# Cross-attention's output projections two tiles ahead of the self-attention turns, and an earlier split of the query weights

## What is computed

```python
x = x + xattn(layernorm(x), ctx)      # 16 heads of 32, q from x, k and v from ctx, softmax, output projection Wo
x = x + attn(layernorm(x))            # qkv projection, rms norm of q and k per head, softmax, projection Wproj
x = x + ffn(layernorm(x))             # token mixing, 9 expert paths, one chosen per token, layernorm
```

## Time and profile before

| | us |
|---|---|
| median of 3 runs | 804.55 (803.83 to 805.03) |
| the profiled execution | 803.47 |
| its span in the trace | 801.9 |
| TensorE matmul busy | 756.4 (94%) |
| VectorE / ScalarE / GpSimd busy | 388.9 / 336.3 / 190.5 |

### The profile page before, as it was taken

One profiled execution on the slowest core, in us unless ns is written; L12 is line 12 of the kernel. 1 busy time (PEld: TensorE's weight loads), 2 busy tenths in 40 slices (PEclk: granted clock), 3 DMA queues, 4 the chain that ended last, 5 costly groups with the idle time before them and its releaser, 6 DMA issues. The chain is left out here.

```text
span 801.9 us, 20594 instructions
## 1 busy us (share of the span) xinstructions
PE 756.4 (94%) x8258; PEld 590.4 (74%) x8258; DVE 388.9 (48%) x941; ACT 336.3 (42%) x690; POOL 190.5 (24%) x246
## 2 busy tenths in 40 slices
PE   5999999999999999999999996699999989999994
PEld 4777778777877887788778774587888766777673
DVE  5644333452444343334433545566667665633446
ACT  4435443544445444435443453334454545521210
POOL 0001010010010010100100202555777760692002
PEclk9999999999999999999999998899999989999998
DMA  8201111011001101110121015120000022100011
GB/s 327 81 36 54 53 54 54 1 52 52 17 36 52 52 0 52 52 52 0 52 52 43 9 52 159 23 73 2 1 0 0 1 68 80 40 0 1 1 54 52
DMA packets 9464, 36.95 MB, mean 46 GB/s; under 512 B 2633, under 2 KB 2889, under 8 KB 6482
## 3 DMA queue, kind: packets, MB, share of 16 engines
q1 hardware_dynamic: 9426, 36.42, 13.4%
HBM read 34.32 MB, written 2.10 MB: 45 GB/s over the span
## 5 line engine op out<-in xcount | busy, mean ns | idle before, releaser
L94 PE MATMUL pj<-W_hi 128*128 128x512 f32 x512 | 209.0, 408 | 9.7 <-DVE W_lo L594 9.7
L96 PE MATMUL pj<-W_lo,W_hi 128*128 128x512 f32 x512 | 200.9, 392 | 0.0
L95 PE MATMUL pj<-W_hi,W_lo 128*128 128x512 f32 x512 | 200.0, 391 | 0.0
L94 PEld LDWEIGHTS pj<-W_hi 128*128 128x128 f32 x512 | 96.6, 189 | 41.0 <-issue 22.6
L96 PEld LDWEIGHTS pj<-W_lo,W_hi 128*128 128x128 f32 x512 | 96.5, 188 | 21.5
L95 PEld LDWEIGHTS pj<-W_hi,W_lo 128*128 128x128 f32 x512 | 96.9, 189 | 17.9
L235 POOL COPY q_b<-Q_T 128x128 f32 (+1 forms) x32 | 9.3, 292 | 415.7 <-PE tp L358 349.0
L492 ACT ACTIVATE K<-pj,bk 128x512 f32<-128x512 f32 x64 | 44.2, 690 | 135.8 <-PE pj L96 135.8
L654 DVE CUSTOM_DVE_ANT_0 m_flat<-sc,mask 128x257 f32<-128x257 f32 x64 | 25.3, 424 | 117.7 <-PE tp L358 94.3
L507 ACT ACTIVATE p_flat<-m_flat,nmax 128x257 f32<-128x257 f32 x128 | 63.8, 501 | 24.6 <-DVE nmax L654 24.5
L499 ACT ACTIVATE V<-pj 128x512 f32<-128x512 f32 x64 | 38.3, 598 | 73.6 <-PE pj L96 71.8
(11 more groups left out here) (271 smaller groups left out, 1337.8 us busy)
## 6 DMA issues: line engine op xcount, KB each, us to landing
raw<-ctx_dram SPq DMA_DIRECT2D x15, 1024.0 KB, 4.8
raw<-w_dram SPq DMA_DIRECT2D x6, 768.0 KB, 4.8
raw<-w_dram SPq DMA_DIRECT2D x4, 1024.0 KB, 4.8
x_nat<-x_dram SPq DMA_DIRECT2D x2, 1024.0 KB, 12.2
out_dram<-raw SPq DMA_DIRECT2D x8, 256.0 KB, 2.1
raw<-wk_dram SPq DMA_DIRECT2D x2, 512.0 KB, 5.7
p_flat<-ctx_dram SPq DMA_DIRECT2D x2, 512.0 KB, 6.9
m_flat<-wv_dram SPq DMA_DIRECT2D x1, 1024.0 KB, 10.3
```

The costliest lines, as they stand in the source:

```text
L94: eng.matmul(out, a_hi, b_hi, start=first, stop=False)
L95: eng.matmul(out, a_lo, b_hi, start=False, stop=False)
L96: return eng.matmul(out, a_hi, b_lo, start=False, stop=last)
```

## The change

- LEAD = 2: `wo_proj` runs for tile it + 2 in turn it. Turn 0 holds `wo_proj` of tiles 0, 1 and 2, turns 1 to 5 that of tiles 3 to 7, turns 6 and 7 none. `o_split` and `o_rest` move with it (tile it + 3 in turn it). Tiles 1 to 3 get halves of their own in `xm_hi`, `xm_lo`, free at that time, and tiles 1, 2 and 3 the banks pw[1], pa[0] and pa[1].
- The low half of tile 1 is made by VectorE (`o1_rest`) instead of GpSimd.
- `x1_stats` is cut in two: `take_x1(t)` (the add into `x_nat`) for tile it + 2, and the statistics for tile it. In turn 0 VectorE's order is: low half of tile 1, take 0, statistics 0, take 1, `weight_split(2)`, take 2.
- In turn 2 the Q projection comes before the q and k transposes on TensorE. In turn 1 VectorE's second `mean_squares` and the V evacuation come before the head norm of q.
- Turns 6 and 7 are written out on TensorE and VectorE; turns 3 to 7 on ScalarE and GpSimd.
- In the last pair of cross-attention, the split of Wq moves ahead: on ScalarE before the first V evacuation, on VectorE between the two `mask_max`.

```diff
@@ cross_attention, scalar, pair
                 k_evac(n, 3)
+                if last:
+                    weight_split(1, 8 * (NPAIR - 1) + 4)
                 v_evac(n, 0)
...
                 v_evac(n, 2)
-                if last:
-                    weight_split(1, 8 * (NPAIR - 1) + 4)
                 v_evac(n, 3)
@@ cross_attention, vector, pair
                 mask_max(n, 0)
+                if last:
+                    weight_split(1)
                 mask_max(n, 1)
...
                 pt_evac(n, 0)
-                if last:
-                    weight_split(1)
@@ second block
+LEAD = 2
...
+        def wo_bank(t):
+            if isinstance(t, int) and t <= LEAD + 1:
+                return (pw[0][:, :], pw[1][:, :], pa[:, 0, :], pa[:, 1, :])[t]
+            return pw[0][:, :]
+        def o_halves(t):
+            if isinstance(t, int) and t <= LEAD + 1:
+                cols = slice(t * P, (t + 1) * P)
+                return o_first if t == 0 else (xm_hi[:, :, cols], xm_lo[:, :, cols])
+            return o_hi[:, :, :], o_lo[:, :, :]
@@ gpsimd, body
-                if has(it, -1):
-                    o_rest(it + 1)
+                if has(it, -LEAD - 1):
+                    o_rest(it + LEAD + 1)
@@ tensor
-                    elif has(it, 0):
-                        eng.wait_ge(x1_made, it + 1)
+                    elif has(it, -LEAD):
+                        eng.wait_ge(x1_made, it + LEAD + 1)
...
-                if has(it, 0):
-                    wo_proj(it)
                 if isinstance(it, int) and it in (1, 2):
                     z2_transposes(it - 1)
+                if isinstance(it, int) and it == 0:
+                    for t in range(LEAD):
+                        wo_proj(t)
+                if has(it, -LEAD):
+                    wo_proj(it + LEAD)
                 if has(it, 3):
                     out_proj(it)
-                if has(it, 2):
+                if isinstance(it, int) and it == 2:
+                    qkv(it, 0)
                     qk_transposes(it)
-                if has(it, 1):
-                    qkv(it, 0)
+                else:
+                    if has(it, 2):
+                        qk_transposes(it)
+                    if has(it, 1):
+                        qkv(it, 0)
@@ scalar, body
-                if has(it, -1):
-                    o_split(it + 1)
+                if first:
+                    for t in range(1, LEAD + 2):
+                        o_split(t)
+                elif has(it, -LEAD - 1):
+                    o_split(it + LEAD + 1)
@@ vector, body
-                x1_stats(it, ch)
+                if isinstance(it, int) and it == 0:
+                    o1_rest()
+                    take_x1(0)
+                    x1_stats(0, ch)
+                    take_x1(1)
+                    weight_split(2)
+                    take_x1(LEAD)
+                else:
+                    if has(it, -LEAD):
+                        take_x1(it + LEAD)
+                    x1_stats(it, ch)
...
-                if has(it, 1):
+                if isinstance(it, int) and it == 1:
+                    k_evac(it)
+                    mean_squares(it, 1)
+                    v_evac(it)
+                    head_norm(it - 1, 0)
+                elif has(it, 1):
                     k_evac(it)
                     head_norm(it - 1, 0)
                     mean_squares(it, 1)
```

More of the change, by code:

```diff
@@ L911, in steps @@
                 body(it)
-            with eng.Fori(3, NT) as i:
+            with eng.Fori(3, NT - LEAD) as i:
                 body(i)
-        def wo_bank(it):
-            return pw[1] if isinstance(it, int) and it == 1 else pw[0]
+            for it in range(NT - LEAD, NT):
+                body(it)
+        def wo_bank(t):
[7 more added lines that the diff above has]
+            return o_hi[:, :, :], o_lo[:, :, :]
         def k_bank(it):
@@ L1041, in _ @@
                               ALU.add).then_inc(ov_last, 1)
-            o_rest(1)
+            for t in range(2, LEAD + 2):
+                o_rest(t)
             norm1(0)
             eng.wait_ge(small_in, 4 * 16)
-            for it in range(1, 4):
+            for it in range(1, NT):
                 body(it)
-            with eng.Fori(4, NT - 1) as i:
-                body(i)
-            body(NT - 1)
             head_norm(1, NT - 2)
@@ L1097, in z2_transposes, with wo_proj @@
                 mm.then_inc(z2T_done, 1)
-            def wo_proj(it):
-                if isinstance(it, int) and it == 0:
+            def wo_proj(t):
+                if isinstance(t, int) and t == 0:
                     eng.wait_ge(wlo, 1)
-                need(eng, olo_made, it)
-                if has(it, 2):
-                    eng.wait_ge(qk_out, 2 * (it - 1))
-                halves = o_first if isinstance(it, int) and it == 0 else (o_hi, o_lo)
-                project(wo_bank(it)[:, :], *halves, 0).then_inc(wo_done, 1)
+                elif isinstance(t, int) and t == 1:
+                    eng.wait_ge(olo1_made, 1)
+                else:
+                    eng.wait_ge(olo_made, t - 1)
+                if has(t, LEAD + 2):
+                    eng.wait_ge(qk_out, 2 * (t - LEAD - 1))
+                project(wo_bank(t), *o_halves(t), 0).then_inc(wo_done, 1)
             def out_proj(it):
@@ L1210, in body @@
                     weighted_sum(it)
-                if not isinstance(it, int) or it == 2:
+                if not isinstance(it, int) or it >= 2:
                     z2_transposes(it)
@@ L1351, in o_split @@
             def o_split(t):
-                if not (isinstance(t, int) and t == 1):
+                if not (isinstance(t, int) and t <= LEAD + 2):
                     eng.wait_ge(wo_done, t)
-                eng.activation(o_hi[:, :, :], O_T[:, :, bass.ds(t * P, P)], ACT.Copy).then_inc(ohi_made, 1)
+                eng.activation(o_halves(t)[0], O_T[:, :, bass.ds(t * P, P)], ACT.Copy).then_inc(ohi_made, 1)
             def z2_make(it):
@@ L1472, in _ @@
             eng.wait_ge(ov_last, 1)
-            with eng.Fori(3, NT - 1) as i:
-                body(i)
-            body(NT - 1)
+            for it in range(3, NT):
+                body(it)
             qk_evac(NT)
@@ L1629, in body @@
                     q_evac(it)
-                if isinstance(it, int) and it == 0:
-                    weight_split(2)
                 if has(it, 2):
@@ L1660, in body @@
                     assert ch.k == PER_STEP
-                    count["at"] += (NT - 3) * PER_STEP
+                    count["at"] += (NT - LEAD - 3) * PER_STEP
                 else:
```

24 lines of the change are left out of this document (15 added, 9 removed).

## The result

| | before | after |
|---|---|---|
| median (range, runs) | 804.75 (803.83 to 805.03, 4) | 794.59 (793.65 to 797.43, 4) |
| profiled execution / its span | 803.47 / 801.9 | 793.65 / 791.7 |
| mean granted clock of the span | 0.979 | 0.990 |

The ratio after to before is 0.9882, 95% interval 0.9855 to 0.9908: faster by 1.2%. A second series gave 794.99 against 802.90, ratio 0.9883 (0.9854 to 0.9912). So the gain lies between 8 and 10 us; 7.1 had been forecast, and the forecast time, 797.4, is 2.4 to 2.8 us above what came. The kernel before itself moved by 1.85 us from one series to the next, and the profiled execution of the kernel after is the fastest of its four, with the highest clock: the other three had 0.983 to 0.986.

A forecast was written before the change was run, and what follows sets the result against it. TensorE was taken as the bound nearly everywhere, except for idle time and slow clock at the second block's start. Gains 1.0 + 3.6 + 2.5 = 7.1 us gave 797.4 us, inner range 795.5 to 799.5, outer 794.3 to 801.5.

The forecast's parts named there:

- second rival: Second block's front: later hole doesn't throttle, or the loop's unexplained 1.7 us wait vanishes; 796.0 to 794.3 us; chance 0.15.
- Part 1: Last pair of cross-attention: moved weight split lets the final weighted sum start earlier at no cost; gain 1.0 us.
- Part 2, the gapless start and z at 7.7: Second block's head: TensorE runs 24.2 us without stopping; first normalised tile z ready at 7.7 us instead of 9.5.
- third rival: Second block's head: VectorE's split starts before GpSimd's shift, so var_eps stalls again; 798.5 to 799.7 us; chance 0.07.
- Part 2, the new hole: Before the second Q projection: TensorE idles 4.0 us for a take behind Wp_lo, then low clock; whole front gains 3.6 us.
- Part 3: Turns 6 and 7: each loses a 2.88 us projection but waits for o_lo; together they gain 2.5 us.
- first rival: Turns 6 and 7 stay at 18.4 us and the clock falls in one or both; 801 to 803 us; chance 0.18.
- Code fetch: Written-out turns add 0, upper bound one or two waits of 1.7 us; the loop's first-turn wait stays.
- The rival's waits: Turns 6 and 7: three code waits of 1.72 us per turn, 10.3 us in all, giving 807.7 us; chance 0.06.

The follow-up runs named there:

- p1_only: Kernel before with only the moved split of the query weights in the last pair of cross-attention: 801.84 us against 802.90, ratio 0.9976.
- lead1: Kernel after with the output projections one tile ahead instead of two: 796.24 us, ratio 0.9907.
- split_first: Kernel after with VectorE's first weight split in turn 0 put back ahead of the take of tile 1: 796.02 us, ratio 0.9913.
- take_first: Kernel after with VectorE's take of projection 4 moved ahead of the Wp_lo split: 792.29 us, ratio 0.9879.
- norm_before_v: Kernel after with the head norm in turn 1 back ahead of the second mean_squares and V evacuation: 796.76 us, ratio 0.9908.
- z_first: take_first plus, in turn 1, z2_hi ahead of ScalarE's split of Wp and z2_lo ahead of VectorE's head norm: 789.12 us, ratio 0.9820.
- after_again: Kernel after, unchanged, run and profiled a second time: 794.99 us, ratio 0.9883.
- p2_only: Kernel after with both splits of Wq in the last pair of cross-attention back in their old places: 795.73 us, ratio 0.9903.
- late_order: Kernel after with VectorE making the halves of o ahead of the head norm in turns 6 and 7: 795.91 us, ratio 0.9914.
- best: z_first and late_order together, with the latter's order also in the step behind turn 7: 789.11 us, ratio 0.9825.
- no_loop: Kernel after with turns 3 to 5 also written out on TensorE and VectorE: 798.13 us, ratio 0.9937.
- transposes_first: Kernel after with the q and k transposes back ahead of the Q projection on TensorE in turn 2: 796.58 us, ratio 0.9912.

## Why the prediction was right, and where it was not

In the profile of the kernel after, the terms that the change touches came out as worked out, each within about 0.4 us. The number owes something to the width of the range: 794.59 and 794.99 lie below the inner range of 795.5 to 799.5, which had most of the chance, and 0.3 and 0.7 us above the lower end of the outer one. They are where the second rival (the front goes better, 0.15) had put them, but only in part by its causes: the wait in turn 3 shrank by 0.9 us, but the clock did fall behind the hole, and the rest came from code that the sum had not counted.

**Part 1, 1.0 us: right.** 1.20 us of wait became 0.16, and 1.06 us went from the medians with p1_only. The ScalarE half cost nothing, as taken.

**Part 2, the gapless start and z at 7.7: right.** z's activation ended 7.5 us after the start, var_eps took 0.19 us, and Q was there 11.7 us after the start, without a wait. (The prediction counts from 486.0, 0.16 us ahead of the first matmul.) The margin of the third rival, about 0.2 us between shift and the split, was 0.18, and it held. The start was not quite gapless: TensorE waited 0.43 us for VectorE in front of projection 4. lead1 shows that the third projection was the needed cover (1.75 us of wait without it), and split_first that the stall of GpSimd beside the split moves the second hole by its 1.8 us.

**Part 2, the new hole: right in place, cause and size.** Forecast 24.2 to 28.2 us after the start, measured 23.9 to 28.27; its row says 4.34 us against 4.0. take_first and norm_before_v move it by the durations of what is queued ahead of the take (-2.19 and +1.19). The low clock behind it cost 1.3 us in one profile and 2.5 in the other; 1.4 had been taken, with 0 to 2.9 as bounds. By the Trainium skill (TensorE: Matmul & The Clock Gate, section "HAM oscillation") a long enough hole between bursts puts the array back to half rate. Behind the holes of 4.3 us the trace agrees (granted 0.50 from 514 to 516 us); behind the shorter ones of 2.15 and 1.53 in take_first and z_first the matmuls stayed at 0.39 us. Turn 3 began 42.98 us after the start, forecast 43.0: the gain of 3.6 was 3.5. In after_again it began at 44.21, since the clock stayed low for longer: that the forecast is met to a tenth is luck of the execution, that it is met to a microsecond is not.

**Part 3, 2.5 us: right in kind, 0.4 too much.** The wait for o_lo is 1.42 us, as forecast from the step behind turn 7; lead1 shows it turn by turn. The two turns gave 2.08 us. Most of the 0.4 can be placed: behind the wait `out_proj` took 2.90 us to the next transposes instead of 2.81, in both turns, and the transposes of turn 6 took 0.97 instead of 0.80; the prediction had carried over the distance up to `out_proj` only. The first rival, that they give all back and the clock falls, didn't come: the clock held at 1.00 through the turns.

**Code fetch, taken as 0 with the old wait staying: wrong twice, in small.** In turn 3 the wait without a releaser went from 1.72 to 0.82 us in the kernel after, and to 0.54 or 0.55 in others, which gave 0.9 us that the second rival had as its possible end; in lead1 turn 3 has 0.49 and 1.72 us. And in part of the kernels turn 7 has one of its own (0.55 in p2_only and take_first, 0.83 in split_first, 0.82 in late_order, 1.10 in best). In the first three it cost next to nothing, as the wait for o_lo behind it was 0.46 us instead of 1.42; in the last two, where that wait was short already, it cost its length. (The 1.94 us of the earlier trace rows are also put down to issue, but z_lo was ready 0.1 us ahead of that matmul, at 498.52: that is a wait for z_lo.) The step that said "fresh code in turns 0 to 2 shows no such wait, so I add 0" was a weak one: no_loop shows that fresh code of the full turns does wait, for 0.99 and 1.42 us, and with the clock that fell behind it for 3.1 us of time. The rival's waits are real. Their number was exaggerated: none or one in a turn instead of three, of 0.5 to 1.4 us, and 1.72 once more only in lead1.

**The mis-sized term: the code that isn't touched.** The sum gave it 0, and it gave 2.61 us in the first pair of profiles, nearly the whole 3.1 us by which the first series' gain exceeds the forecast, and 1.83 with the profile of after_again. The table below has the time from `out_proj` behind turn 7 to the end of the span, in the same code everywhere but for best's last step:

| kernel | from, us | to the end, us |
|---|---|---|
| before | 628.05 | 173.9 |
| p1_only | 626.44 | 174.1 |
| after | 620.46 | 171.2 |
| after_again | 621.48 | 172.0 |
| p2_only | 620.58 | 171.9 |
| z_first | 616.73 | 171.4 |
| take_first | 616.95 | 171.5 |
| split_first | 621.78 | 171.6 |
| lead1 | 623.27 | 171.7 |
| norm_before_v | 623.65 | 171.9 |
| best | 616.73 | 171.9 |
| no_loop | 623.84 | 172.0 |
| late_order | 619.68 | 173.8 |
| transposes_first | 621.01 | 176.5 |

The kernels differ in nothing there but in the moment at which they arrive. Ten of the twelve profiles with the change have 171.2 to 172.0, the two without it 173.9 and 174.1, so most of the gain is no accident of one profile. Shown is that stretches of low clock of 3 to 7 us, and once one of over 10, account for it: the hidden projection had one before, in p1_only and in late_order, and not in after, after_again, p2_only, z_first and transposes_first.

```profile
736.90:738.90 2.00, 1.68 (x5) 1.13 (x5) 1.30 (x3) 1.12 (x2) 0.00 (x0) 0.71 0.00 0
```

```profile
728.00:730.00 2.00, 1.45 (x6) 1.00 (x7) 1.19 (x2) 1.18 (x3) 0.00 (x0) 1.00 0.00 0
```

```profile
728.70:730.70 2.00, 1.68 (x5) 1.25 (x5) 1.30 (x3) 1.12 (x2) 0.00 (x0) 0.70 0.00 0
```

(Before, after, late_order; stretches of 2 us, columns as in rows 1: the granted clock is 0.71, 1.00 and 0.70.) Why the clock falls in one execution and not in another with the same work ahead was not settled by any run. Part of it goes with the kernel: all four executions of late_order have a mean clock of 0.983, and most of the kernel before 0.979. Whether the place of the block's other holes in time decides it is a guess that no experiment here tested.

## What to carry to other kernels

Before moving work to cover a wait, ask what is queued behind the next shared bank: here the new hole was a take behind a 2.3 us weight split, foreseeable from durations alone, and shortening it (z_first) was worth 3.8 to 5.0 us in the profiles, as much as the cover itself (3.5). A projection that fills an engine also hides the others' chains, so taking it out of a turn gives back its length less those chains: read them in a step that already runs without it. Where a kernel has places at which the clock may fall, 2 to 3 us of 800 can come or go in code that nobody touched; put that into the range, and judge an edit by the rows at its place.

## What the runs showed of the hardware

- Code run for the first time is, by the best reading of the traces, not free even without branches: two waits of 0.99 and 1.42 us when three loop turns were written out, in bursts of small matmuls, and 5 more packets on the instruction queue. The size of such a wait differs from execution to execution of one kernel (0.82 and 0.55 us at the same place in after and after_again).
- Behind waits of 2.15 and 1.53 us TensorE's clock stayed at its upper level, behind 4.3 us it fell to 0.50. Yet the same waits of 0.78 and 0.32 us were followed by a fall in one kernel and none in another, so the wait just ahead is not all that counts.
- A 128x1 operation of GpSimd takes 0.19 us alone. When it began 0.3 us after VectorE's 128x2048 subtraction it took 2.00 us and ended with it; with the subtraction moved behind a take, so that it began 1.3 us after the operation, it took 0.19. Beside that take, which reads one of its operands from a bank of TensorE's results, GpSimd's shift took 0.27 us, as it did with VectorE idle.
